# A two-layer decoder in one launch: the routing of the second set of experts moved into the last head group of the cross attention, token transfers issued one to a step, first tiles and weights staged ahead

## The reference

```python
x  = LN(x + attention(x))                  # 16 heads of 128, rope            stage a
x  = LN(x + cross_attention(x, ctx))       # 32 heads of 16, axial rope       stage b
x  = LN(x + moe(x))                        # 32 experts, top 4, capacity 80,
                                           # shared expert                    stages cd, m, cc
x  = LN(x + attention(x))                  # 16 heads of 32, causal           stage d
x  = LN(x + cross_attention(x, ctx))       # 16 heads of 128, rms of q and k  stage e
x  = LN(x + moe(x))                        # 8 experts, top 2, no drops       stages r, n, fc

# moe of the last sublayer
logits = x @ gate_w.T                      # 8 columns
w, idx = top_2(logits); w = softmax(w)
for e in range(8):
    out += w_e * (silu(x @ gate_proj[e].T) * (x @ up_proj[e].T)) @ down_proj[e].T   # F = 352
```

## Time and profile before

| | us |
|---|---|
| median of three runs | 3529.71 |
| the runs | 3530.47, 3529.71, 3528.15 |
| profiled execution, its own time | 3531.17 |
| its span in the trace | 3529.2 |
| TensorE busy | 3179.0 (90%) |
| VectorE busy | 2078.1 (59%) |
| GpSimd busy | 1443.5 (41%) |
| ScalarE busy | 1277.4 (36%) |

### The profile page before, as it was taken

The page is one execution under the profiler, slowest core; times in us unless marked ns, Lnnn a source line. Parts: engine busy times, 40 slices in busy tenths (PEclk is TensorE's granted clock), DMA queues, the critical chain, the costliest instruction groups (busy, mean ns, idle before and its releaser), DMA issues. The chain is left out here.

```text
span 3529.2 us, 59019 instructions
## 1 busy us (share of the span) xinstructions
PE 3179.0 (90%) x21140; PEld 2651.9 (75%) x21140; DVE 2078.1 (59%) x3732; ACT 1277.4 (36%) x3276; POOL 1443.5 (41%) x1470
## 2 busy tenths in 40 slices
PE   6999999999969999799896999599999999759992
PEld 5887878878847777677685777488888888748881
DVE  4666566676646666421164777466666678335566
ACT  2333333333346666201102333244444444224340
POOL 3454343444322434300162222355555566344445
PEclk9999999999979999889898999799999999679996
DMA  4001016023210100349663111411101000156664
GB/s 167 20 17 50 0 35 229 0 93 114 90 68 29 54 26 20 143 137 343 195 151 104 37 44 35 144 35 32 35 23 35 12 23 12 55 206 220 220 222 155
DMA packets 138293, 320.20 MB, mean 91 GB/s; under 512 B 18473, under 2 KB 30505, under 8 KB 135586
## 3 DMA queue, kind: packets, MB, share of 16 engines
q1 hardware_dynamic: 121058, 280.90, 23.5%
q0 software_dynamic: 15360, 36.25, 3.9%
q10 hardware_dynamic: 1728, 1.07, 0.1%
HBM read 234.21 MB, written 98.04 MB: 94 GB/s over the span
## 5 line engine op out<-in xcount | busy, mean ns | idle before, releaser
L377 POOL TENSOR_TENSOR a_sq<-a_tq,a_sinq 128x256 f32<-128x256 f32 x128 | 149.8, 1190 | 355.6 <-DVE a_tq L448 355.6
L377 POOL TENSOR_TENSOR a_sk<-a_tk,a_sink 128x256 f32<-128x256 f32 x128 | 123.7, 985 | 90.0 <-DVE a_tk L448 90.0
L343 ACT COPY a_probT<-bank 128x512 f32<-128x512 f32 x64 | 37.5, 585 | 327.5 <-PE bank L653 327.5
L390 POOL TENSOR_TENSOR e_sk<-e_tk 128x512 f32<-128x512 f32 x64 | 66.7, 1042 | 210.3 <-DVE e_tk L475 210.3
L330 ACT ACTIVATE a_sm<-a_sm,a_nmax 128x128 f32<-128x128 f32 x256 | 99.8, 391 | 121.4 <-DVE a_nmax L535 121.4
L335 ACT ACTIVATE e_prob<-bank,e_nb,e_rq 128x128 f32<-128x128 f32 x256 | 113.7, 455 | 82.5 <-DVE e_nb L540 82.5
L881 ACT ACTIVATE b_prob<-bank,b_nb 128x128 f32<-128x128 f32 x512 | 139.0, 386 | 10.0 <-DVE b_nb L1077 10.0
L975 POOL TENSOR_TENSOR d_prob<-d_prob,d_nmax 128x1024 f32<-128x1024 f32 x32 | 64.0, 1999 | 181.7 <-DVE d_nmax L1072 181.7
L2203 POOL TENSOR_TENSOR n_wu_lo<-nw_wu,n_wu_hi 128x1408 fp32r<-128x1408 f32 x23 | 74.1, 3223 | 143.4 <-DVE n_wu_hi L2247 143.4
L470 DVE TENSOR_TENSOR a_kr<-a_kr,a_sk 128x512 f32<-128x512 f32 x64 | 66.4, 1038 | 88.9 <-POOL a_sk L377 88.9
L1074 DVE TENSOR_REDUCE b_nmax<-bank 128x8 f32<-128x1024 f32 x64 | 77.7, 1214 | 67.4 <-PE bank L1213 66.7
(11 more groups left out here) (507 smaller groups left out, 10669.1 us busy)
## 6 DMA issues: line engine op xcount, KB each, us to landing
packed<-all_zero SPq DMA_DIRECT2D x32, 1024.0 KB, 8.0
cw_wg<-in_c_wg SPq DMA_DIRECT2D x32, 512.0 KB
cw_wu<-in_c_wu SPq DMA_DIRECT2D x32, 512.0 KB
cw_wd<-in_c_wd SPq DMA_DIRECT2D x32, 512.0 KB
nw_wg<-in_f_wg SPq DMA_DIRECT2D x23, 704.0 KB
nw_wu<-in_f_wu SPq DMA_DIRECT2D x23, 704.0 KB
nw_wd<-in_f_wd SPq DMA_DIRECT2D x23, 512.0 KB
n_xe<-packed SPq DMA_DIRECT2D x46, 256.0 KB, 2.7
```

Of the source, the lines that this page charges most:

```text
L343: nc.scalar.copy(probT[:], pP[:, :]).then_inc(act_pt, 1)
L377: step = nc.gpsimd.tensor_tensor(o, i, s, ALU.mult)
L390: nc.gpsimd.tensor_tensor(sk[:], tk[:], tk[:], ALU.mult).then_inc(g_k, 1)
```

## The change

1. **Routing inside e.** A new class `SpreadRouter` holds the routing's buffers, and `wide_attention` takes it as `router`. In the last head group the twelve middle batches are written out instead of looped. From batch 2 on, batch b routes tile r = b-2 (`routed`): TensorE transposes it between the Q/K and the V projections, ScalarE copies it after the exponentials, TensorE finds its logits after the V projection and, for even r from 2 on, counts the pair before; VectorE copies logits and counts and places the pair before the rms scaling of K, and selects at the end of the batch for odd r; the K transposes wait for the logits' copy, since they share a bank. GpSimd sends two transfers a batch from batch 5 on, 22 in all.
2. **End of routing.** `end_of_routing` takes the place of `spread_routing`: it transposes, selects and places what is left (tiles 14 and 15, pairs 6 and 7), sends the last 10 transfers, and works out the table with one multiply and one reduction in place of eight chained additions. SyncE loads the first x tiles of n in this block, those of the first set after all sends.
3. **Staged weights and first tiles.** One buffer for three weight matrices and one for a first x tile are shared by the stages. a's q, k, v and its first tile are loaded in the very first block; b's q, k, v, o and first tile near the end of a; the shared expert's three near the end of b; d's q, k, v at the end of cc, issued by ScalarE; e's q, k, v near the end of d. First tiles of d and e are loaded at their own stage's start.
4. **One transfer to a step in b.** `PLAN_8` spreads the eight sends of a pair over the eight steps: 0 to 3 in the odd batch, 4 to 7 in the next even one. `late_routing` sends 20 where it sent 16. TensorE's output passes are grouped a little otherwise.
5. **combine.** The last shared tile is added after its gathers' accumulation. The buffers of m live inside `base`.

The diff, cut to its core:

```diff
@@ wide_attention, each_unit
+                if router and g == G - 1:
+                    for b in range(2, B - 2):
+                        slot(g, b, b % 2)
+                else:
+                    with engine.Fori(0, B // 2 - 2) as i:
...
@@ wide_attention, SyncE
+                if ahead and g == G - 1 and is_batch(b, B - 2):
+                    for n in "kvo":
+                        sp.wait_ge(w_lo[n], rows_of[n] * G)
...
+                    ahead(sp)
@@ wide_attention, ScalarE, after the exponentials
+                r = routed(g, b)
+                if r is not None:
+                    router.take_x(act, r, pB)
@@ wide_attention, GpSimd
+                sends = router and g == G - 1 and b >= 5
+                if sends:
+                    router.send(pool, (b - 5) // 2, 2 * ((b - 5) % 2))
                 if not last:
                     project(u + 1, 1 - par)
+                if sends:
+                    router.send(pool, (b - 5) // 2, 2 * ((b - 5) % 2) + 1)
@@ wide_attention, VectorE, between the copy of v and kr
+                if r is not None:
+                    take_routing(r)
...
+            def take_routing(r):
+                if counted(r) is not None:
+                    router.take_counts(dve, counted(r), pB)
+                router.take_logits(dve, r, pB)
+                if counted(r) is not None:
+                    router.place(dve, counted(r))
@@ wide_attention, VectorE, end of slot
+                if r is not None and r % 2:
+                    router.select(dve, r // 2)
@@ wide_attention, TensorE, slot
+                if r is not None:
+                    pe.wait_ge(v_yn, done(r))
+                    router.turn_x(pe, r, pB)
+                if not last:
                     pe.wait_ge(v_v, done(u))
                     project("v", pV, s_hi, s_lo, *following_unit, 1 - par, pe_v)
+                if r is not None and not last:
+                    route(r)
...
                 if not last:
+                    if r is not None:
+                        pe.wait_ge(router.v_l, r + 1)
                     turn_k(u + 1)
@@ narrow_attention, GpSimd
-                    if isinstance(e, int) and b % 2 and b >= 5:
-                        router.send(pool, b // 2 - 2, e)
+                    if isinstance(e, int) and (b % 2, e >= 4) in ((1, False), (0, True)) and b >= 5:
+                        router.send(pool, (b - 1) // 2 - 2, e)
@@ PLAN_8
-        ["x", ("o2", 8, 10), "s", "p", ("o2", 10, 12)],
+        ["x", "s", "p", ("o2", 8, 12)],
...
-    "pool": [["c"], [], ["n"], ["q"], [0, 1], ["zl", "k", 2], [3, 4, 5], [6, 7]],
+    "pool": [["c", 4], [5], ["n", 6], ["q", 7], [0], ["zl", "k", 1], [2], [3]],
@@ SpreadRouter
+    def place(self, dve, p):
...
+        for n in range(2):
+            step(vec.tensor_tensor(self.carry[:, b + n + 1], self.carry[:, b + n], self.counts[:, 1, n], ALU.add))
+        step(vec.tensor_tensor(self.pos[:], self.counts[:, 0], self.carry[:, pair], ALU.add))
+        step(vec.tensor_tensor(self.prod[:], self.hot[:, :, pair], self.pos[:].unsqueeze(1).to_broadcast([P, K, 2, NE]), ALU.mult))
+        step(vec.tensor_reduce(self.rowf[:, pair].rearrange("p b k -> p k b"), self.prod[:], AX.X, ALU.add))
+        vec.tensor_copy(self.target[:, pair], self.rowf[:, pair]).then_inc(self.v_p, 1)
@@ end_of_routing, SyncE
             sp.wait_ge(tabled, 2)
             for w in range(2):
                 weights.load(sp, weights.number(sp, 0, w), w)
+                if w == 0:
+                    sp.wait_ge(router.sent, 16 * K * B)
+                weights.load_x(sp, router.packed.rearrange("(t r) d -> t r d", r=P), weights.place(sp, 0, w), w)
@@ end_of_routing, VectorE
-            for e in range(NE):
-                step(vec.tensor_tensor(first[:, e + 1:e + 2], first[:, e:e + 1], npair[:, e:e + 1], ALU.add))
+            step(vec.tensor_tensor(summed[:], upto[:], npair[:].unsqueeze(1).to_broadcast(each), ALU.mult))
+            step(vec.tensor_reduce(first[:, 1:NE + 1], summed[:], AX.X, ALU.add))
@@ combine, ScalarE
+                for n, used in (("q", part.pe_g), ("k", part.pe_u), ("v", part.pe_o)):
+                    act.wait_ge(used, done(part.COUNT - 1))
+                    ahead(act, n)
@@ decoder
-        wide_attention(nc, "a", psum, ident, x, x1, of("a_"), rope=True, background=zero_rows)
+        wide_attention(nc, "a", psum, ident, x, x1, of("a_"), staged_a, head_a, rope=True, background=zero_rows, ahead=fetch_b,
+                       head_ready=True)
...
-                spread_routing(nc, "r", psum, tri, ones, ident, xall, w, packed2, 8, weight, rows, weights, NP2)
+                end_of_routing(nc, "r", psum, router, weight, rows, weights, NP2)
```

More of the change, by code:

```diff
@@ L654, in slot @@
                 step.then_inc(pe_pt, 1)
+                if r is not None and last:
+                    route(r)
                 if not last:
@@ L1676, in _ @@
         def _(sp):
-            part.load(sp)
             prefetch(sp)
@@ L1681, in _ @@
         def _(pool):
+            for n in range(router.K, 2 * router.K):
+                router.send(pool, LAST - 2, n)
             for p in (LAST - 1, LAST):
@@ L1833, in _ @@
-            step(vec.tensor_tensor(full[:], carry[:, B].unsqueeze(2).to_broadcast([P, NE, NE]), limit[:], ALU.is_gt))
+            vec, step = nc.vector, router.step
+            router.take_counts(dve, LAST - 1, pC[0])
+            router.place(dve, LAST - 1)
+            each = [P, NE, NE]
+            step(vec.tensor_scalar(limit[:], iota[:, 0:NE].unsqueeze(1).to_broadcast(each), float(PAIR), None, ALU.mult))
+            step(vec.tensor_tensor(limit[:], limit[:], region[:].unsqueeze(2).to_broadcast(each), ALU.add))
@@ new lines, in _ @@
+            step(vec.tensor_tensor(upto[:], iota[:, 0:NE].unsqueeze(2).to_broadcast(each), iota[:, 0:NE].unsqueeze(1).to_broadcast(each),
+                                   ALU.is_ge))
+            step(vec.memset(first[:, 0:1], 0.0))
+            for n in range(2):
+                router.take_logits(dve, B - 2 + n, pL[n])
+            router.select(dve, LAST)
+            vec.tensor_tensor(apart[:], router.top[:, :, 1], router.top[:, :, 0], ALU.subtract).then_inc(v_c, 1)
+            router.take_counts(dve, LAST, pC[1])
@@ L2135, in refill @@
                     store(i, n)
-            for w in range(2):
-                load_x(place(0, w), w)
             with sp.Fori(0, ROUNDS - 1) as i:
@@ L2329, in _, with combine @@
             down(*LAST)
-def combine(nc, name, base, result, rows, weight, x_dst, K, shared=None):
+def combine(nc, name, base, result, rows, weight, x_dst, K, shared=None, ahead=None):
     R = 4
@@ L2365, in _ @@
         def _(sp):
-            if shared:
-                part.load(sp)
             for n in range(R):
```

418 lines of the change are left out of this document (246 added, 172 removed), and 4 rows, old and new, of the table PLAN_8.

## The result

| | before | changed |
|---|---|---|
| median of four runs, us | 3530.09 | 3481.05 |
| lowest to highest | 3528.15 to 3531.84 | 3477.42 to 3485.08 |
| profiled execution, span | 3529.2 | 3480.8 |

The ratio is 0.9861, with a 95% interval of 0.9844 to 0.9879: 49 us less. All later runs came from chips on which the kernel before takes 3499 to 3504 us. There the changed kernel measured 3467.95 against 3502.24, ratio 0.9902 (0.9886 to 0.9919), 34 us less.

A forecast was written before the change was run, and what follows sets the result against it. It took TensorE as full in e's last group, and routing as filling the stretch behind e. Terms: -44.6 + 25.6 - 8 - 15.5 = -42.5 us, from 3531.17 to 3488.7, median 3487; range 3467 to 3510, holding 80%.

The forecast's parts named there:

- VectorE in e: In e's last group, VectorE's added small operations lose 1 us for each of five pairs: 5 us more, 0 to 12.
- Rival C: VectorE bounds e's last group at the ordinary pace: 12 us in place of 5, plus the sends' 4; 3498 us, 20%.
- The sends in e: The 22 sends in e's last group fit GpSimd's room: taken at nothing, 4 us if that cover is gone.
- Behind e: n's first matmul comes 44.6 us earlier, 37 to 49; SyncE's issues behind the table, not the ten sends, set it.
- b's sends: In b, one send to a step takes back most of TensorE's 9.0 us wait: 8 us less, 0 to 11.
- Openings: Earlier loads shorten waits at the starts of a, b, cc, d and e: 15.5 us less in sum, 0 to 31.
- A: Small chained steps in e run as slowly as at r's end, 0.61 us in place of 0.2: 3523 us, 8%.
- B: Small chained steps in e take 0.8 us each, making the kernel slower than before: 3543 us, 5%.
- D: b's stalls and the waits at stage openings stay, 8 + 10 us less gained: 3505 us, 14%.
- E: Behind e, first x tiles queue behind a set of weights and n starts 8.8 us later: 3496 us, 8%.
- F: Sends in e bind GpSimd above 2.95 us each; at 3.3 it costs 8 us: 3495 us, 3%.
- G: Everything comes back: chain at r's end at 0.2 us a step and full gains at the openings; 3470 us, 8%.

The follow-up runs named there:

- run 1: Changed kernel with the seven placing operations of even batches in e's last group moved behind e_kr: 3450.86 us, ratio 0.9846.
- Run 2: Changed kernel with all 32 transfers of the last expert layer sent behind e, none within its last group: 3479.01 us, ratio 0.9926.
- Run 7: Changed kernel with every first x tile and first set of weights loaded at its own stage's start (a, b, cd, d, e): 3481.11 us, ratio 0.9934.
- run 10: Changed kernel with the table made later on purpose, eight chained additions done twice, 16 steps for 2: 3456.98 us, ratio 0.9877.
- run 8: Changed kernel with placing behind e_kr, and both sets of expert weights issued before the wait for all sends, then x tiles: 3451.47 us, ratio 0.9852.
- run 12: Changed kernel with placing behind e_kr; SyncE waits for sends, loads first x tiles, then first weights; second set in the expert stage: 3446.33 us, ratio 0.9845.
- run 9: Changed kernel with placing behind e_kr; first weights, wait for sends, first x tiles; second set issued in the expert stage: 3448.24 us, ratio 0.9856.
- run 11: Changed kernel with SyncE's wait for all sends put ahead of the first expert weights: 3458.02 us, ratio 0.9881.
- runs 6: The changed kernel, unchanged, measured again on a later chip: 3467.95 us, ratio 0.9902 to the kernel before.

## Why the prediction was right, step by step

The time was forecast at 3487 in a range of 3467 to 3510, and the median is 3481.05; the sum was -42.5, measured -49.0 us. Behind that, terms of both signs were off: the last group and the last norm took 5.8 us more than forecast, the way behind e 8.4 less. That these nearly cancel is luck, and so is the open -5.0 of n.

- **TensorE's price in e** (19.8): right. With VectorE's wait gone, run 1's group is 19.1 us longer than before (203.1 to 184.05).
- **VectorE in e** (5, bound 12): the group has 9.0 us more (212.1 to 203.1). The place was right, placing ahead of `kr`, but I priced the steps' own time. What costs is where they push `e_kr`: into GpSimd's send and two subtractions, 2.34 us a time (3.48 less 1.14). Rival C's 12 was nearer in size, and its reason, VectorE full, was wrong: moving 1.5 us of work by one place ends it.
- **The sends in e** (nothing, bound 4): 3.4 of these 9.0 us, through the same meeting.
- **What holds `e_kr`.** The sends in e last 1.04 to 1.14 us where I priced 0.98, so GpSimd has the room I gave it. The hold has no term in the prediction. Run 2 shows it without the sends: the operation that starts 0.22 us behind the subtraction takes 1.38 us for 0.35 and ends 0.15 behind it (2938.73 against 2938.58). With the sends the held operation has started ahead of the subtraction. In run 1 a cast of 128x4 is held beside the same two, and the steps of 0.17 to 0.19 us beside the send are not. What decides which operation is held was not shown. I had looked at the operations that the change adds, not at those that it moves beside one another.
- **The last norm** (0.8): 3.3 us on the first chip, 1.2 on the later ones, where this stretch varies by 2.9 us between kernels, so what it costs is not shown.
- **Behind e** (-44.6): -53.0. Two steps failed. The chain's pace: 0.61 us was taken from the earlier trace rows, it ran at 0.25; so the table came 16.2 us behind the norm, not 20.9. And the statement that the ten sends "do not set this": they do. The end of the last send was forecast well, 18.7 us behind the norm (3052.1 against 3033.36), and is 19.0. But with the table early the first weights were issued ahead of the last send's start, and its landing, 8 us until SyncE went on, had no term. SyncE's own row of issues, priced at 9.7 us from the earlier trace rows for two sets, takes 2.2 for one when nothing stands before it. On a later chip the kernel before shows how it really was. There SyncE has issued both sets of weights at 3073 and the next stage's x tiles at 3092.94, with GpSimd's last of 32 sends at 3080.57 between:

```profile
3072.28 0.95 SPq L2075 DMA_DIRECT2D nw_wd<-in_f_wd  x2
3092.94 2.49 SPq L2118 DMA_DIRECT2D n_xe<-packed  x4
```

```profile
3080.57 0.97 POOL L1773 DMA_INDIRECT packed<-moe_xall,r_target  x1 [0.30 <-issue]
```

  The row of sends ended the block, in which GpSimd waits for all 32 to land, with 12.4 us behind the last one; on the first chip it is 12.0 (3103.62 to 3115.62), so most likely there too. Run 2 divides the gain behind e: with the routing in e but all 32 sends behind it the way is 52.8 us, 32 less than before (85.2 on a later chip), and moving 22 sends takes 19.8 more. In both it is the row of sends that ends last, so there the earlier table by itself gains nothing.
- **b's sends** (-8): -7.8 on the first chip, 0.0 on the later ones. Right where it was forecast, for a stall that is the chip's.
- **Openings** (-15.5): a -5.4 (4 forecast), a to b -4.9 (5), cc +0.7 on the first chip and -1.4 on the later ones (3.5), d -0.9 (1), e -3.7 (2), and b's first batches -2.7, not forecast: TensorE's granted clock there is higher, at the first chip 0.87 from 1002 to 1012 where it was 0.63 from 1010 to 1020. Run 7 gives 13 us for all but cc by its median. At cc the forecast failed: the wait for weights went, but waits on "issue" in the same stage grew on the first chip from 4.9 to 7.4 us.
- **Rivals.** A and B fell: small steps ran at 0.2 us in e on both sorts of chip. D did not come; on the later chips b's 8 us are missing because the kernel before doesn't lose them there either. E did not come in the changed kernel, whose x tiles are issued when the first weights are through and land in 2.6 us (on a later chip); its mechanism is real, 6.4 us behind one set of weights in run 10 and 6.5 behind two in run 8. F fell: it needs sends over 2.95 us and is priced at 3.3, which no row or run shows; those in e last 1.04 to 1.14. G's first half, the chain at 0.2, came true.

## What to carry to other kernels

When work is added to a full stage, look at what it pushes, not only at what it lasts: an operation that VectorE used to end before GpSimd began can meet it now (here `e_kr`, 3.48 us in place of 1.14), and a table of both engines' starts in one batch shows that beforehand. When several queues end a block (a chain of small steps, a row of scatters and their landing, a row of issues), write the end of each before pricing a gain; here the row of scatters was the last, and bringing weights early made it later (the last one landed after 7.1 to 7.4 us in place of 2.7). A transfer that someone waits for goes ahead of bulk loads that nobody needs yet: run 12 differs from run 9 in that order, and its way to n is 25.6 us in place of 28.2.

## What the runs showed of the hardware

- The same kernel took 3530 us on one chip and 3499 to 3504 on others, at the same granted clock (0.947 and 0.948). Of 27 us, 14 lie in b and 10 in cc, the stages in which GpSimd scatters and gathers beside TensorE's work, where idle time put to "issue" stands on the first chip and not on the later ones (TensorE in b 9.0 us, in cc 4.9); a, m, d, e and n agree within 3 us. Why one chip has these gaps is open.
- The small chained steps at r's end took 0.61 us each on that chip in the kernel before and 0.25 in the changed one, beside the same kind of sends; on a later chip 0.23 in the kernel before. What brought the gaps in the earlier trace rows was not tried.
- SyncE goes on 2.9 to 3.8 us after the start of the last scatter when no weights are in flight (the landing itself comes at 2.7), and 7.6 to 8.1 with a set of weights, 2.1 MB, issued about the same time. Two x tiles of 256 KB each land 5.7 (run 11) to 6.4 us (run 10) after their issue behind such a set and 2.6 to 2.7 without (runs 6 and 12).
- One of the four operations of `e_kr` (128x128), 0.35 us alone, took 1.38 beside GpSimd's subtraction `e_x_lo` (run 2) and 2.23 where a send ran ahead of that (the changed kernel); a cast of 128x4, 0.17 alone, took 1.71 (run 1).
- TensorE's granted clock stood at 0.50 or at 1.00 in 3517 of 3529 windows of 0.25 us, one in each us of the trace of before, and between them in the other 12; a mean such as 0.63 over 10 us mixes the two.
